# Other orders on all engines in a loop's body and its first tile: statistics, exponentials and a weight check moved

## The reference

```python
x = x + attn0(layernorm(x))   # 16 heads, linear: phi = silu + 1, kv = phi(k)^T v, out = phi(q) kv
h = silu(n @ w1.T * s1) * (n @ w2.T * s2)          # n = layernorm(x); w: ternary, 1024 hidden
h = gelu(h @ h1.T * sh1); h = gelu(h @ h2.T * sh2)
x = x + h @ w3.T * s3
x = x + softmax(q k^T / 16) v @ w_out + b_out      # layernorm(x) first, one head over 512 tokens
x = x + tanh(layernorm(x) @ weight @ aux1 @ aux2 + bias)
```

## Time and profile before

| what | us |
|---|---|
| median of 3 runs | 2041.03 (2040.67 to 2041.18) |
| the profiled execution, its own time | 2039.72 |
| its span, first to last instruction | 2037.9 |
| PE busy | 1926.6 (95%) |
| DVE busy | 1328.5 (65%) |
| ACT busy | 817.7 (40%) |
| POOL busy | 409.8 (20%) |

### The profile page before, as it was taken

One profiled execution on the slowest core, in us unless ns is written; L12 is line 12 of the kernel. 1 busy time (PEld: TensorE's weight loads), 2 busy tenths in 40 slices (PEclk: granted clock), 3 DMA queues, 4 the chain that ended last, 5 costly groups with the idle time before them and its releaser, 6 DMA issues.

```text
span 2037.9 us, 27407 instructions
## 1 busy us (share of the span) xinstructions
PE 1926.6 (95%) x10170; PEld 1632.2 (80%) x10170; DVE 1328.5 (65%) x3183; ACT 817.7 (40%) x1286; POOL 409.8 (20%) x344
## 2 busy tenths in 40 slices
PE   7999999999999999999999999999999999999998
PEld 6877887888878888788887888788787887888887
DVE  5676685766857567675676757667576585765347
ACT  3443434344343443434334343343433434344333
POOL 1212030220403113031130311303022030220211
PEclk9999999999999999999999999999999999999999
DMA  9430312313023130221302213031230312313200
GB/s 378 157 105 32 124 32 73 114 42 124 32 73 103 42 135 22 82 93 52 135 21 93 73 62 125 32 100 56 73 114 32 124 34 71 113 42 114 83 21 22
DMA packets 59241, 171.10 MB, mean 84 GB/s; under 512 B 5296, under 2 KB 25520, under 8 KB 58928
## 3 DMA queue, kind: packets, MB, share of 16 engines
q1 hardware_dynamic: 59104, 169.25, 24.2%
HBM read 160.85 MB, written 19.92 MB: 89 GB/s over the span
## 4 chain that ended last, share of the span: by engine, by line
PE 76%; DVE 13%; ACT 5%; POOL 2%; issue 2%; DMA 1%; SPq 1%; ACTq 0%; DVEq 0%
PE ffn_fill L1152 37%; PE att_fill L1083 25%; PE ffn_fill L1083 11%; DVE turned L801 5%; POOL xt_lo L686 2%; DVE turned_b L818 2%; DVE act_lo L840 2%; PE att_fill L1283 1%; DVE xn L720 1%; DVE st L704 1%; PE att_fill L1170 1%; ACT whole L1013 1%; ACT L1044 1%; ACT act_hi L1015 1%; ACT L1013 1%
## 5 line engine op out<-in xcount | busy, mean ns | idle before, releaser
L1152 PE MATMUL ffn_fill<-act_hi,hw 128*128 128x512 f32 x2048 | 804.0, 393 | 1.3 <-DVE act_lo L840 1.3
L1152 PE MATMUL ffn_fill<-act_lo,hw 128*128 128x512 f32 x2048 | 798.7, 390 | 0.0
L1152 PEld LDWEIGHTS ffn_fill<-act_hi,hw 128*128 128x128 f32 x2048 | 384.7, 188 | 78.4 <-DVE act_lo L840 1.8
L1152 PEld LDWEIGHTS ffn_fill<-act_lo,hw 128*128 128x128 f32 x2048 | 384.7, 188 | 76.8
L1013 ACT ACTIVATE whole<-ffn_fill,scales 128x512 f32<-128x512 f32 x256 | 175.9, 687 | 526.9 <-PE ffn_fill L1152 526.4
L840 DVE TENSOR_TENSOR act_lo<-whole,act_hi 128x512 fp32r<-128x512 f32 x256 | 176.5, 689 | 281.8 <-ACT act_hi L1015 281.4
L681 POOL TENSOR_TENSOR act_lo<-whole,act_hi 128x512 fp32r<-128x512 f32 x128 | 166.5, 1301 | 246.1 <-DVE act_hi L836 245.6
L1083 PE MATMUL ffn_fill<-half_hi,w 128*128 128x512 f32 x512 | 202.6, 396 | 2.3 <-issue 2.3
L1083 PE MATMUL ffn_fill<-half_lo,w 128*128 128x512 f32 x512 | 199.8, 390 | 0.0
L1015 ACT ACTIVATE act_hi<-whole 128x512 fp32r<-128x512 f32 x256 | 161.7, 632 | 8.2
L818 DVE STREAM_TRANSPOSE turned_b<-xn_b 32x128 f32<-32x128 f32 x480 | 145.2, 302 | 6.7
...
## 6 DMA issues: line engine op xcount, KB each, us to landing
hw<-scratch_h1T SPq DMA_DIRECT2D x128, 512.0 KB, 3.3
hw<-scratch_h2T SPq DMA_DIRECT2D x128, 512.0 KB, 3.2
...
```

Source lines behind the costliest of these rows:

```text
L1152: last = pe.matmul(bank[:], view(hw[:, j, k, :]), view(moving[:, k, :]), start=k == 0 and half == 0, stop=k == KH - 1 and half == 1)
```

## The change

Only the lists are changed: which step stands where on each engine, and which PSUM bank of its ring a step gets. No instruction is added to or taken from a step. In the body: on DVE the next tile's statistics stand ahead of H5, the normalisation and the transposes one step further ahead, c:DST ahead of G5 and c:DNO ahead of n:NT0a. On ACT c:LT stands ahead of G0, the four exponentials ahead of G3, and c:CF ahead of H0. On PE c:CS1 stands ahead of c:CP0, c:CO3 between the halves of G5, the second c:LT ahead of all of G7 and c:CF's halves each a half step ahead of H0. POOL adds c:CB's bias ahead of the power of n:BST0. SP stores c:CF's tile ahead of H1's weights. In the first tile a:ANO, p:AO and a:LT stand ahead of the look at w12, CHECK0 behind the last m:BT1, and f:TA1 and f:TA2 at the end of DVE's queue ahead of U0; later checks, looks and n:NT move by a step or two.

```diff
 PE_ORDERS = {
     "FIRST": order_from("""
-         WARM24 p:LT p:AKV0 p:AKV1 p:AKV2 p:AKV3 f:FA0 p:AS p:AQ p:AM f:FA1 p:AO a:LT f:FA2 a:AKV0 CHECK0 a:AKV1
-    m:BT0 a:AKV2 a:AKV3 m:BT1 U0 U1 U2 a:AS a:AQ U3 U4 U5 CHECK1 a:AM U6 U7 G0a a:AO G0b G1 G2 G3a FOLD0 G3b G4
+         WARM24 p:LT p:AKV0 p:AKV1 p:AKV2 p:AKV3 f:FA0 p:AS p:AQ p:AM f:FA1 p:AO a:LT f:FA2 a:AKV0 a:AKV1 a:AKV2
+    m:BT0 a:AKV3 m:BT1 CHECK0 U0 U1 U2 a:AS a:AQ U3 U4 U5 CHECK1 a:AM U6 U7 G0a a:AO G0b G1 G2 G3a FOLD0 G3b G4
...
     "BODY": order_from("""
          H5 H6 H7 W0 W1 U0 a:AKV0 U1 a:AKV1 U2 a:AKV2 U3 a:AKV3 U4 U5 a:AS a:AQ U6 a:AM U7 G0a a:AO G0b c:LT G1a
-    c:CV     G1b c:CZ G2 c:CS0 G3a c:CP0 c:CS1 c:CS2 G3b c:CO0 c:CP1 c:CS3 G4a c:CO1 c:CP2 G4b c:CO2 c:CP3 G5
-    c:CO3 G6     G7a c:LT G7b H0a c:CFa H0b c:CFb H1 H2 H3 H4"""),
+    c:CV     G1b c:CZ G2 c:CS0 G3a c:CS1 c:CP0 c:CS2 G3b c:CO0 c:CP1 c:CS3 G4a c:CO1 c:CP2 G4b c:CO2 c:CP3 G5a
+    c:CO3 G5b G6     c:LT G7 c:CFa H0a c:CFb H0b H1 H2 H3 H4"""),
...
 DVE_ORDERS = {
     "FIRST": order_from("""
          p:AST p:ANO PREP0 p:LT p:AKV0 SCALE p:AKV1 p:AKV2 a:ASTa p:AKV3 a:ASTb PREP1 f:TA0 p:AS p:AQ p:AM
-    LOOK00     a:ANO LOOK01 p:AO a:LT m:BST0 m:BST1 f:TA1 CHECK0 m:BNO0 f:TA2 a:AKV0 m:BT0 m:BNO1 a:AKV1 a:AKV2
-    a:AKV3 m:BT1     U0 LOOK10 U1 U2 LOOK11 a:AS LOOK12 LOOK13 a:AQ U3 U4 U5 CHECK1 a:AM U6 WIDE U7 a:AO n:BST0
+    a:ANO p:AO a:LT m:BST0 m:BST1 a:AKV0 LOOK00 m:BNO0 a:AKV1 LOOK01 m:BT0 m:BNO1 a:AKV2 CHECK0 a:AKV3 m:BT1
+    f:TA1 f:TA2     U0 LOOK10 U1 U2 LOOK11 a:AS LOOK12 LOOK13 a:AQ U3 U4 U5 CHECK1 a:AM U6 WIDE U7 a:AO n:BST0
...
     "BODY": order_from("""
-         H5 a:AST H6 a:ANO a:Ta H7 a:Tb W0 W1 c:CSTa U0 a:AKV0 U1 a:AKV1 c:CSTb U2 a:AKV2 U3 a:AKV3 U4 U5 a:AS
-    a:AQ U6 a:AM U7 c:CNO a:AO n:BST0 c:LT c:CQ G0 n:BST1 c:CV G1 c:CZ c:CS0 G2 c:CP0 c:CS1 c:CS2 c:CO0 G3
-    c:CP1 c:CS3 c:CO1 c:CP2 G4 c:CO2 c:CP3 n:BNO0 c:CO3 G5 c:DSTa c:DSTb n:NT0a G6 c:DNO n:NT0b c:LT G7 n:NTL0
+         a:AST H5 a:ANO a:Ta H6 a:Tb H7 W0 W1 c:CSTa U0 a:AKV0 U1 a:AKV1 c:CSTb U2 a:AKV2 U3 a:AKV3 U4 U5 a:AS
+    a:AQ U6 a:AM U7 c:CNO a:AO n:BST0 c:LT c:CQ G0 n:BST1 c:CV G1 c:CZ c:CS0 G2 c:CS1 c:CP0 c:CS2 c:CO0 c:CP1
+    c:CS3 G3     c:CO1 c:CP2 G4 c:CO2 c:CP3 n:BNO0 c:CO3 c:DSTa c:DSTb G5 c:DNO n:NT0a G6 n:NT0b c:LT G7 n:NTL0
     n:BNO1     c:CF H0 n:NT1a H1 n:NT1b H2 n:NTL1 H3 H4"""),
...
 ACT_ORDERS = {
     "BODY": order_from("""
-         H5 H6 H7 a:T U0 a:AKV0 U1 a:AKV1 U2 a:AKV2 U3 a:AKV3 U4 U5 a:AQ U6 a:AM U7 G0 c:LT G1 c:CV c:CZ G2
-    c:CS0 c:CP0 c:CS1 c:CS2 G3 c:CP1 c:CS3 c:CP2 G4 c:CP3 G5 G6 c:LT n:NT0 G7 H0 c:CF H1 H2 n:NT1 H3 H4"""),
+         H5 H6 H7 a:T U0 a:AKV0 U1 a:AKV1 U2 a:AKV2 U3 a:AKV3 U4 U5 a:AQ U6 a:AM U7 c:LT G0 G1 c:CV c:CZ G2
+    c:CS0 c:CS1 c:CP0 c:CS2 c:CP1 c:CS3 G3 c:CP2 G4 c:CP3 G5 G6 c:LT n:NT0 G7 c:CF H0 H1 H2 n:NT1 H3 H4"""),
...
 POOL_ORDERS = {
     "BODY": order_from("""
-         a:AST a:AB a:T U0 U1 c:CST U2 U3 U4 U5 U6 U7 n:BST0 c:CB n:BST1 c:DST c:CF"""),
+         a:AST a:AB a:T U0 U1 c:CST U2 U3 U4 U5 U6 U7 c:CB n:BST0 n:BST1 c:DST c:CF"""),
...
 SP_ORDERS = {
     "BODY": order_from("""
-    H5 H6 H7 G0 G1 G2 G3 G4 G5 G6 G7 H0 H1 c:CF H2 H3 H4"""),
+         H5 H6 H7 G0 G1 G2 G3 G4 G5 G6 G7 H0 c:CF H1 H2 H3 H4"""),
```

More of the change, by code:

```diff
@@ L149 @@
 PLAN = steps_from("""
-    H5 a:AST H6 H7 a:ANO W0 a:AB a:T W1 U0 c:CST a:AKV0 U1 a:AKV1 U2 a:AKV2 U3 a:AKV3 U4 U5 a:AS a:AQ U6 a:AM U7
-    c:CNO a:AO n:BST0 G0 c:LT G1 G2 G3 G4 G5 c:CB c:CQ n:BST1 c:CV c:CZ c:CS0 c:CP0 c:CS1 c:CS2 c:CO0 c:CP1
-    c:CS3 c:CO1 c:CP2 c:CO2 c:CP3 n:BNO0 c:CO3 c:DST n:NT0 G6 c:DNO c:LT G7 n:NTL0 n:BNO1 c:CF H0 n:NT1 H1 H2
+    H5 a:AST H6 a:ANO H7 W0 a:AB a:T W1 U0 c:CST a:AKV0 U1 a:AKV1 U2 a:AKV2 U3 a:AKV3 U4 U5 a:AS a:AQ U6 a:AM U7
+    c:CNO a:AO G0 G1 G2 G3 G4 c:CB n:BST0 c:LT c:CQ n:BST1 c:CV c:CZ c:CS0 c:CS1 c:CP0 c:CS2 c:CO0 c:CP1 c:CS3
+    c:CO1 c:CP2 c:CO2 c:CP3 n:BNO0 c:CO3 c:DST G5 c:DNO n:NT0 G6 c:LT G7 n:NTL0 n:BNO1 c:CF H0 n:NT1 H1 H2
     n:NTL1 H3 H4""")
@@ L227 @@
     WARM24 p:AST p:ANO p:LT PREP0 p:AKV0 p:AKV1 SCALE p:AKV2 a:AST p:AKV3 f:FA0 PREP1 p:AB p:AS f:TA0 p:AQ p:AM
[L228 to L231, removed]
+    a:ANO f:FA1 p:AO a:LT m:BST0 m:BST1 a:AKV0 f:FA2 LOOK00 m:BNO0 a:AKV1 LOOK01 m:BT0 m:BNO1 a:AKV2 a:AKV3
+    CHECK0 m:BT1 f:TA1 f:TA2 U0 LOOK10 U1 U2 LOOK11 a:AS LOOK12 a:AQ LOOK13 U3 a:AB U4 U5 CHECK1 a:AM U6 WIDE U7
+    a:AO n:BST0 G0 n:BST1 G1 G2 LOOK20 G3 n:BNO0 FOLD0 TAKE0 G4 CHECK2 LOOK30 G5 n:NT0 G6 CHECK3 LOOK40 G7
+    n:NTL0 n:BNO1 H0 CHECK4 H1 LOOK50 LOOK60 n:NT1 H2 H3 CHECK5 CHECK6 n:NTL1 H4""")
 BODY = PLAN
@@ L247 @@
     "FIRST": order_from("""
-         WARM24 p:LT p:AKV0 p:AKV1 p:AKV2 p:AKV3 f:FA0 p:AS p:AQ p:AM f:FA1 p:AO a:LT f:FA2 a:AKV0 CHECK0 a:AKV1
-    m:BT0 a:AKV2 a:AKV3 m:BT1 U0 U1 U2 a:AS a:AQ U3 U4 U5 CHECK1 a:AM U6 U7 G0a a:AO G0b G1 G2 G3a FOLD0 G3b G4
-    G5a     CHECK2 G5b G6 CHECK3 G7 H0a CHECK4 H0b H1 H2a CHECK5 CHECK6 H2b H3 H4"""),
+         WARM24 p:LT p:AKV0 p:AKV1 p:AKV2 p:AKV3 f:FA0 p:AS p:AQ p:AM f:FA1 p:AO a:LT f:FA2 a:AKV0 a:AKV1 a:AKV2
+    m:BT0 a:AKV3 m:BT1 CHECK0 U0 U1 U2 a:AS a:AQ U3 U4 U5 CHECK1 a:AM U6 U7 G0a a:AO G0b G1 G2 G3a FOLD0 G3b G4
+    G5a     CHECK2 G5b G6 CHECK3 G7 H0 H1a CHECK4 H1b H2 H3a CHECK5 CHECK6 H3b H4"""),
     "BODY": order_from("""
          H5 H6 H7 W0 W1 U0 a:AKV0 U1 a:AKV1 U2 a:AKV2 U3 a:AKV3 U4 U5 a:AS a:AQ U6 a:AM U7 G0a a:AO G0b c:LT G1a
-    c:CV     G1b c:CZ G2 c:CS0 G3a c:CP0 c:CS1 c:CS2 G3b c:CO0 c:CP1 c:CS3 G4a c:CO1 c:CP2 G4b c:CO2 c:CP3 G5
-    c:CO3 G6     G7a c:LT G7b H0a c:CFa H0b c:CFb H1 H2 H3 H4"""),
+    c:CV     G1b c:CZ G2 c:CS0 G3a c:CS1 c:CP0 c:CS2 G3b c:CO0 c:CP1 c:CS3 G4a c:CO1 c:CP2 G4b c:CO2 c:CP3 G5a
+    c:CO3 G5b G6     c:LT G7 c:CFa H0a c:CFb H0b H1 H2 H3 H4"""),
     "END": order_from("""
@@ L263 @@
          p:AST p:ANO PREP0 p:LT p:AKV0 SCALE p:AKV1 p:AKV2 a:ASTa p:AKV3 a:ASTb PREP1 f:TA0 p:AS p:AQ p:AM
-    LOOK00     a:ANO LOOK01 p:AO a:LT m:BST0 m:BST1 f:TA1 CHECK0 m:BNO0 f:TA2 a:AKV0 m:BT0 m:BNO1 a:AKV1 a:AKV2
-    a:AKV3 m:BT1     U0 LOOK10 U1 U2 LOOK11 a:AS LOOK12 LOOK13 a:AQ U3 U4 U5 CHECK1 a:AM U6 WIDE U7 a:AO n:BST0
-    n:BST1 G0 G1 G2 LOOK20     G3 TAKE0 n:BNO0 G4 CHECK2 LOOK30 G5 n:NT0a G6 CHECK3 LOOK40 n:NT0b n:NTL0 n:BNO1
-    G7 CHECK4 LOOK50 LOOK60 H0     CHECK5 CHECK6 n:NT1a H1 n:NT1b H2 n:NTL1 H3 H4"""),
+    a:ANO p:AO a:LT m:BST0 m:BST1 a:AKV0 LOOK00 m:BNO0 a:AKV1 LOOK01 m:BT0 m:BNO1 a:AKV2 CHECK0 a:AKV3 m:BT1
+    f:TA1 f:TA2     U0 LOOK10 U1 U2 LOOK11 a:AS LOOK12 LOOK13 a:AQ U3 U4 U5 CHECK1 a:AM U6 WIDE U7 a:AO n:BST0
+    n:BST1 G0 G1 G2 LOOK20     G3 TAKE0 n:BNO0 G4 CHECK2 LOOK30 n:NT0a G5 n:NT0b G6 CHECK3 LOOK40 G7 n:NTL0
+    n:BNO1 H0 CHECK4 LOOK50 LOOK60     n:NT1a H1 CHECK5 CHECK6 n:NT1b H2 n:NTL1 H3 H4"""),
     "BODY": order_from("""
-         H5 a:AST H6 a:ANO a:Ta H7 a:Tb W0 W1 c:CSTa U0 a:AKV0 U1 a:AKV1 c:CSTb U2 a:AKV2 U3 a:AKV3 U4 U5 a:AS
-    a:AQ U6 a:AM U7 c:CNO a:AO n:BST0 c:LT c:CQ G0 n:BST1 c:CV G1 c:CZ c:CS0 G2 c:CP0 c:CS1 c:CS2 c:CO0 G3
-    c:CP1 c:CS3 c:CO1 c:CP2 G4 c:CO2 c:CP3 n:BNO0 c:CO3 G5 c:DSTa c:DSTb n:NT0a G6 c:DNO n:NT0b c:LT G7 n:NTL0
+         a:AST H5 a:ANO a:Ta H6 a:Tb H7 W0 W1 c:CSTa U0 a:AKV0 U1 a:AKV1 c:CSTb U2 a:AKV2 U3 a:AKV3 U4 U5 a:AS
+    a:AQ U6 a:AM U7 c:CNO a:AO n:BST0 c:LT c:CQ G0 n:BST1 c:CV G1 c:CZ c:CS0 G2 c:CS1 c:CP0 c:CS2 c:CO0 c:CP1
+    c:CS3 G3     c:CO1 c:CP2 G4 c:CO2 c:CP3 n:BNO0 c:CO3 c:DSTa c:DSTb G5 c:DNO n:NT0a G6 n:NT0b c:LT G7 n:NTL0
     n:BNO1     c:CF H0 n:NT1a H1 n:NT1b H2 n:NTL1 H3 H4"""),
@@ L281 @@
     "FIRST": order_from("""
-         PREP0 p:LT p:AKV0 p:AKV1 p:AKV2 p:AKV3 PREP1 p:AQ p:AM a:LT LOOK00 LOOK01 a:AKV0 a:AKV1 m:BT0 a:AKV2
+         PREP0 p:LT p:AKV0 p:AKV1 p:AKV2 p:AKV3 PREP1 p:AQ p:AM a:LT a:AKV0 LOOK00 a:AKV1 LOOK01 m:BT0 a:AKV2
     a:AKV3 m:BT1 U0 LOOK10 U1 U2 LOOK11 LOOK12 LOOK13 a:AQ U3 U4 U5 a:AM U6 U7 G0 G1 G2 LOOK20 G3 G4 LOOK30 G5
-    G6     LOOK40 G7 n:NT0 LOOK50 LOOK60 H0 H1 H2 n:NT1 H3 H4"""),
+    n:NT0 G6     LOOK40 G7 H0 LOOK50 LOOK60 H1 H2 n:NT1 H3 H4"""),
     "BODY": order_from("""
-         H5 H6 H7 a:T U0 a:AKV0 U1 a:AKV1 U2 a:AKV2 U3 a:AKV3 U4 U5 a:AQ U6 a:AM U7 G0 c:LT G1 c:CV c:CZ G2
-    c:CS0 c:CP0 c:CS1 c:CS2 G3 c:CP1 c:CS3 c:CP2 G4 c:CP3 G5 G6 c:LT n:NT0 G7 H0 c:CF H1 H2 n:NT1 H3 H4"""),
+         H5 H6 H7 a:T U0 a:AKV0 U1 a:AKV1 U2 a:AKV2 U3 a:AKV3 U4 U5 a:AQ U6 a:AM U7 c:LT G0 G1 c:CV c:CZ G2
+    c:CS0 c:CP0 c:CS1 c:CS2 c:CP1 c:CS3 G3 c:CP2 G4 c:CP3 G5 G6 c:LT n:NT0 G7 c:CF H0 H1 H2 n:NT1 H3 H4"""),
     "END": order_from("""
```

## The result

The changed kernel takes 2005.29 us (median of 4 runs, 2003.38 to 2006.33), the kernel before 2041.11 beside it (4 runs): a ratio of 0.9822, 95% interval 0.9805 to 0.9839. The forecast was 2006, with 1986 to 2016 around it. The profiled execution of the changed kernel is its fastest, 2003.38.

A forecast was written before the change was run, and what follows sets the result against it. TensorE bounds the kernel, the other engines only through their queues' order. Terms of −2.16 us a turn (−30.2 over 14 turns) and −5.0 for the first tile gave 2004.5, as a median 2005.8 us; range 1986 to 2016.

The forecast's parts named there:

- statistics ahead of H5: Loop, DVE: a:AKV0's wait for POOL's low half goes (−1.18), W0 waits 0.70 longer; net −0.48 us a turn.
- c:LT ahead of G0: Loop, ACT: copies before G0 have c:LT's low halves ready, so c:CV's wait goes; −1.51 us a turn.
- exponentials: Loop: c:CS1 ahead of c:CP0 gains 1.37, G3 behind c:CS3 gives 1.12 back at c:CO2; −0.25 us a turn.
- c:DST, c:LT, c:CF: Loop: second c:LT's wait for the normalisation goes (−1.53), a new wait of 1.61 comes at c:CF; +0.08 us a turn.
- The wait at c:CF: Loop, TensorE: c:LT's low half, behind n:NT0 and G6 on DVE, is late; true loss 1.61, row about 1.45 us.
- First tile: Before the loop: normalisation fills DVE's idle ahead of the look at w12, U0's second half starts at 45.1; −5.0 us.
- TensorE's unbroken G and H work: First tile: the later moves of checks lie under this work; no gain or loss counted.
- 1968 to 1990: Rival, loop: new waits absent at c:CO2 (1990, chance 0.10), at c:CF (1983, 0.06) or at both (1968, 0.03).
- the rival: Loop: c:CF's new wait of 1.61 us a turn does not come; 1983 us, chance 0.06.
- Without c:CO2's: Rival, loop: c:CO2's new wait of 1.12 us a turn does not come; 1990 us, chance 0.10.
- Slower, by the next tile's load: Rival, loop: early statistics wait for the next tile's DMA; 2071 us if it lands at 1010, chance 0.04.
- the prediction's estimate: Loop, ACT: by the skill's rule alone, two table switches less a turn save 74 us; time about 1965.

## Why the prediction was right

**By terms.** Taken from the starts and ends of TensorE's steps, mean of 13 turns:

| term | forecast | measured | made of |
|---|---|---|---|
| statistics ahead of H5 | −0.48 | −0.57 | a:AKV0 −1.17 and −0.13 in the step, W0 +0.73 |
| c:LT ahead of G0 | −1.51 | −1.62 | c:CV −1.51 and −0.11 in the step |
| exponentials | −0.25 | −0.23 | c:CP0 −1.36 and −0.02 in the steps, c:CO2 +1.15 |
| c:DST, c:LT, c:CF | +0.08 | +0.27 | c:LT −1.54 and −0.27 in the step, c:CF +1.96 and +0.12 |
| sum | −2.16 | −2.15 | the turn: −2.18 |

The mechanisms are the forecast's, each at its place: W0 1.67 (forecast 1.64), c:CP0 0.20 (0.20), c:CO2 1.16 (1.12). Runs of their own bear out the statistics (alone −0.57) and c:CF's wait (its removal). No run moves c:LT ahead of G0, or c:DST with c:DNO, alone: those gains rest on the waits that are gone from the trace of after. Two sizes were off and nearly cancelled, so that the sum came this close is partly luck.

*The wait at c:CF* was to be 1.45 and is 1.79. DVE's row of work came as laid out, 0.14 late: c:LT's low half was put at 1105.0, with c:CO2 at 1088.72; c:CO2 stands at 1065.74 here, so that is 1082.02, and it started at 1082.16. TensorE was there 0.2 earlier than worked out. The step took c:LT's transposes at 1.08 from the earlier trace rows; there they waited for the normalisation block by block, and unhindered they take 0.8 to the next step's start.

*What stands behind a wait* was left out. The forecast counted a wait as its row plus 0.16. The first matmul after one is longer as well: at W0 above 0.39, and the next start 0.22 on, against 0.28 and 0.12 for the others. So each wait costs 0.11 more in the step behind it, and a wait block by block 0.27. That is what the table has as "in the step", and why the move of c:LT's low halves alone gave 2.08 for a wait of 1.79: 1.79 + 0.16 + 0.12 = 2.07.

**First tile: two misses against each other.** U0 began at 43.34, 5.75 earlier, its second half at 44.66 (forecast 45.1) and U1 at 46.53 (forecast 46). But U2 came at 48.93, only 3.9 earlier than its 52.85 before. The term took U0's and U1's time from the trace of before. After, TensorE was idle 2.72 ahead of U0, and the granted clock fell; the same view over the idle and over the stretch:

```profile
40.50:43.34 2.84, 0.12 (x3) 0.03 (x2) 2.69 (x8) 0.60 (x1) 0.00 (x0) 1.00 0.97 378
44.30:47.71 3.41, 3.36 (x8) 2.47 (x8) 1.12 (x3) 1.72 (x3) 0.00 (x0) 0.50 1.22 502
```

From U0's start to U2's it took 5.59 in place of 3.76, so 1.83 lost. In the execution of before, the clock fell at 34.25, behind the wait of 4.2, in work with another idle of 2.32 still to come ahead of U0. The old first tile can lose the clock at U0 as well: in the run with the statistics alone, PE's line at U0 and the stretch behind it are

```profile
48.88 0.54 PE L1083 MATMUL ffn_fill<-half_hi,w 128*128 128x512 f32 x1 [2.31 <-issue]
```

```profile
49.18:52.59 3.41, 3.41 (x9) 2.64 (x8) 0.06 (x1) 1.72 (x3) 0.00 (x0) 0.50 1.02 387
```

It did so in one of four executions with the old first tile, and in all nine with the new one. On the other side the forecast took the later moves of the first tile for nothing. One of them was not. In the kernel before, PE's line at the second half of H0:

```profile
111.41 0.50 PE L1152 MATMUL ffn_fill<-act_hi,hw 128*128 128x512 f32 x1 [1.34 <-DVE act_lo L840]
```

G7's low half stood there behind n:NTL0 and n:BNO1 on DVE. The change puts G7 first, the wait goes, and H5 comes 1.6 earlier for it (1.34 + 0.16 + 0.11): −3.9 − 1.6 = −5.5 in this pair of executions, 4.7 by the medians of all. "TensorE's unbroken G and H work" was the sentence that failed, and that −5.0 came out near is luck.

**The rest.** The last tile's 0.3 was not forecast. The half-clock stretch in it is 8.98 long before and 6.96 after, which may be the reason; no run tests it. That the median lies above the profiled execution was forecast at 1.3 and is 1.9. Together these make 2005.3 for 2005.8.

**The rivals.** The new waits came, so 1968 to 1990 did not; the runs above made these cases on purpose. Without c:CF's wait it is 1974.2, where the rival said 1983. A turn lost 2.08 by that and not 1.61, which is 6.6 us in all, and the rest is that one profiled execution stands against a median (1.9 in the changed kernel). "Without c:CO2's" was wrong as a case: G3's place moves that wait to c:CO3 and gains 0.2 a turn, not 1.12. Slower, by the next tile's load: the loop has no wait of the statistics for a load, and H5 still has 1.00 of idle ahead of it. The Trainium skill's rule in "ScalarE: Activation LUTs", section "Table sets: the hidden batching unit", would have given about 1965 by the prediction's estimate. The runs don't bear it out here: with six loads in place of four the usual turn was 0.2 shorter, because what the grouping moves, G3, is what is late. The load is 1.28 as that page's "What ACT_TABLE_LOAD costs" says; the drain of 1.38 it adds shows neither before nor after: G0's load above starts 0.01 behind the end of the copy ahead of it (1034.01 + 1.09), and G0's Gelu follows at 1036.41, 0.02 behind the load.
